# Counting two search rows in one packed pass, cutting GpSimd's projection low parts into pieces, and staging eleven weight tiles in block 0

## What is computed

```python
xn = layernorm(x)
s  = silu(xn @ Wg_a.T)
_, idx = top_k(-abs(s), k=1376)          # the half of each row nearest zero
s  = s.at[rows, idx].set(0.0)
s  = (s * (xn @ Wu_a.T)) @ Wd_a.T
g  = silu(((silu(xn @ Wg_b.T)) * (xn @ Wu_b.T)) @ Wd_b.T)
out = x + s * g
```

## Time and profile before

| | |
|---|---|
| median of 3 runs | 2782.26 us (2779.91 to 2783.34) |
| the profiled execution | 2784.59 us, its span 2782.8 us |
| TensorE busy in the span | 2753.9 us (99%) |
| VectorE busy | 2307.4 us (83%) |
| ScalarE busy | 1352.7 us (49%) |
| GpSimd busy | 388.3 us (14%) |
| mean granted clock | 0.996 |
| stages of block 0 on TensorE | A to 255.5 us, B to 489.5 us, BD to 608.4 us, AD from 613.0 us |

### The profile page before, as it was taken

The page is one execution under the profiler, slowest core; times in us unless marked ns, Lnnn a source line. Parts: engine busy times, 40 slices in busy tenths (PEclk is TensorE's granted clock), DMA queues, the critical chain, the costliest instruction groups (busy, mean ns, idle before and its releaser), DMA issues. The chain is left out here.

```text
span 2782.8 us, 31374 instructions
## 1 busy us (share of the span) xinstructions
PE 2753.9 (99%) x12204; PEld 2281.1 (82%) x12204; DVE 2307.4 (83%) x3002; ACT 1352.7 (49%) x1386; POOL 388.3 (14%) x161
## 2 busy tenths in 40 slices
PE   9999999999999999999999999999999999999999
PEld 7778888878788888888878888888887888888887
DVE  7676999999967698998986678999897767999971
ACT  4234998332444477631144557671115446776110
POOL 5565443044400000000020000000011000000000
PEclk9999999999999999999999999999999999999999
DMA  6898888579766555556656655555666664555564
GB/s 235 308 328 286 293 288 280 211 251 357 255 193 196 181 188 192 189 203 219 249 190 195 192 180 190 195 196 194 240 223 195 193 196 173 195 196 193 189 233 170
DMA packets 135097, 614.28 MB, mean 221 GB/s; under 512 B 12752, under 2 KB 12752, under 8 KB 89168
## 3 DMA queue, kind: packets, MB, share of 16 engines
q1 hardware_dynamic: 134992, 612.94, 63.2%
HBM read 492.31 MB, written 120.59 MB: 220 GB/s over the span
## 5 line engine op out<-in xcount | busy, mean ns | idle before, releaser
L632 PE MATMUL ps<-w_split,hid_ring 128*128 128x512 f32 x4096 | 935.2, 390 | 6.8 <-ACT hid_buf L1136 4.6
L632 PEld LDWEIGHTS ps<-w_split,hid_ring 128*128 128x128 f32 x4096 | 769.4, 188 | 171.5 <-issue 7.9
L1380 DVE TENSOR_SCALAR_CACHE_REDUCE ranks<-key_buf,cand 128x2752 int16<-128x2752 f32 x248 | 762.9, 3076 | 5.8
L961 ACT ACTIVATE signs_row<-key_buf,cand 128x2752 bf16<-128x2752 f32 x248 | 642.6, 2591 | 191.6 <-DVE cand L1389 182.0
L877 PE MATMUL ps<-xnT,w_split 128*128 128x512 f32 x1376 | 535.3, 389 | 0.0
L876 PE MATMUL ps<-xnT,w_split 128*128 128x512 f32 x1376 | 535.3, 389 | 0.0
L875 PE MATMUL ps<-xnT,w_split 128*128 128x512 f32 x1376 | 535.3, 389 | 0.0
L1206 POOL TENSOR_TENSOR w_split<-w_raw,w_split 128x1024 fp32r<-128x1024 f32 (+2 forms) x118 | 290.2, 2467 | 377.3 <-ACT w_split L928 137.0
L875 PEld LDWEIGHTS ps<-xnT,w_split 128*128 128x128 f32 x1376 | 258.3, 188 | 53.7
L876 PEld LDWEIGHTS ps<-xnT,w_split 128*128 128x128 f32 x1376 | 258.3, 188 | 53.6
L877 PEld LDWEIGHTS ps<-xnT,w_split 128*128 128x128 f32 x1376 | 258.3, 188 | 53.3
(11 more groups left out here) (146 smaller groups left out, 2907.0 us busy)
## 6 DMA issues: line engine op xcount, KB each, us to landing
w_split<-split SPq DMA_DIRECT2D x272, 1024.0 KB, 4.8
split<-w_split SPq DMA_DIRECT2D x72, 1024.0 KB, 6.8
w_raw<-w_a SPq DMA_DIRECT2D x100, 512.0 KB, 4.2
w_raw<-t_dram SPq DMA_DIRECT2D x78, 512.0 KB, 3.3
w_raw<-w_b SPq DMA_DIRECT2D x42, 512.0 KB, 4.9
w_extra_raw<-t_dram SPq DMA_DIRECT2D x42, 512.0 KB, 3.6
t_dram<-t_buf SPq DMA_DIRECT2D x20, 1024.0 KB, 8.6
w_extra_raw<-w_a SPq DMA_DIRECT2D x30, 512.0 KB, 3.6
```

Of the source, the lines that this page charges most:

```text
L632: ins = pe.matmul(ps[:, 2 * t + half, :], h, w[:, half * TB:(half + 1) * TB], start=(first and n == 0), stop=last and stop)
L961: act.activation(signs_row[:, :], keys[:, t, :], ACT.Sign, bias=cand_f[:, t:t + 1], scale=-1.0, accum_out=counts[:, t:t + 1]).then_inc(act ...
L1380: dve.tensor_scalar(ranks[:, :], keys[:, t, :], cand_f[:, t:t + 1], 0.0, ALU.is_lt, ALU.add, accum_out=counts[:, t:t + 1]).then_inc(sel_st ...
```

## The change

Three things are changed.

1. **Packed counts.** Row 0's comparison (key < candidate) writes 4096 or 0 into `ranks` and takes no sum. Row 1's comparison (key >= candidate) adds this to its own 1 or 0, in one `scalar_tensor_tensor` that takes the sum along. Two further steps of one column separate the two counts, by rounding to a multiple of 4096. `product_b` of a chunk moves from ahead of its first round into that round, between these steps and the wait for ScalarE's counts. The 31st round moves from BD into B: `TWO_AFTER` has nine chunks, (1, 3, 6, 8, 10, 12, 14, 16, 18), where it had eight.
2. **GpSimd in BD of block 0.** The low parts of BD's tiles are made in four pieces of 256 columns, and their waits for `hid_lo` (`LOWS_GATE`) are gone. In stage B the low parts stay whole, with their waits for `cand_ready`.
3. **Staging.** 11 tiles are staged where it were 14, one after every fourth tile of A where it was every third. So BD of block 0 splits 11 of its tiles itself, where it were 8.

```diff
-TWO_AFTER = (1, 4, 6, 9, 11, 14, 16, 19)
+TWO_AFTER = (1, 3, 6, 8, 10, 12, 14, 16, 18)
-LOWS_ROUND = 5
-assert ROUNDS_B + 1 == ROUNDS and LOWS_MASKS[-1][-1] == NJ
+assert ROUNDS_B == ROUNDS and LOWS_MASKS[-1][-1] == NJ
-STAGED = 14
-LOWS_GATE = {14: 14, 15: 14, 16: 15, 17: 18, 18: 18, 19: 19, 20: 19, 21: 22}
+STAGED = 11
 def stage_at(m):
-    s = (m - 3) // 3
-    return s if m % 3 == 0 and 0 <= s < STAGED else None
+    s = (m - 3) // 4
+    return s if m % 4 == 3 and 0 <= s < STAGED else None
...
-                    if j == 0:
-                        count(ROUNDS_B)
...
-                elif BD0 + STAGED <= m < AD0:
-                    pool.wait_ge(hid_lo, LOWS_GATE[m - BD0])
...
-                pool.tensor_tensor(w_lo[q][:, 0:w], w_raw[q][:, 0:w], w_hi[q][:, 0:w].bitcast(F32),
-                                   ALU.subtract).then_inc(lo_ready, 1)
+                piece = w // 4 if BD0 <= m < AD0 else w
+                for c in range(0, w, piece):
+                    cols = slice(c, c + piece)
+                    ins = pool.tensor_tensor(w_lo[q][:, cols], w_raw[q][:, cols], w_hi[q][:, cols].bitcast(F32), ALU.subtract)
+                ins.then_inc(lo_ready, 1)
...
-                def search_round(n):
+                def search_round(n, product=None):
...
-                    for t in range(DVE_ROWS):
-                        if t > 0:
-                            dve.wait_ge(sel_step, done + t)
-                        dve.tensor_scalar(ranks[:, :], keys[:, t, :], cand_f[:, t:t + 1], 0.0, ALU.is_lt, ALU.add,
-                                          accum_out=counts[:, t:t + 1]).then_inc(sel_step, 1)
-                    dve.wait_ge(sel_step, done + DVE_ROWS)
+                    dve.tensor_scalar(ranks[:, :], keys[:, 0, :], cand_f[:, 0:1], PACK, ALU.is_lt, ALU.mult).then_inc(sel_step, 1)
+                    dve.wait_ge(sel_step, done + 1)
+                    dve.scalar_tensor_tensor(out=ranks[:, :], in0=keys[:, 1, :], scalar=cand_f[:, 1:2], in1=ranks[:, :],
+                                             op0=ALU.is_ge, op1=ALU.add, accum_out=counts[:, 0:1]).then_inc(sel_step, 1)
+                    dve.wait_ge(sel_step, done + 2)
+                    dve.tensor_scalar(above[:, :], counts[:, 0:1], float(-(I // 2)), PACK_ROUND, ALU.add, ALU.add).then_inc(sel_step, 1)
+                    dve.wait_ge(sel_step, done + 3)
+                    dve.scalar_tensor_tensor(out=counts[:, 1:2], in0=above[:, :], scalar=PACK_ROUND, in1=counts[:, 0:1],
+                                             op0=ALU.subtract, op1=ALU.subtract).then_inc(sel_step, 1)
+                    if product is not None:
+                        product_b(product)
+                    dve.wait_ge(sel_step, done + 4)
                     dve.wait_ge(act_counted, b * (ROUNDS * ACT_ROWS) + n * ACT_ROWS + ACT_ROWS)
...
                 for c, rounds in enumerate(ROUNDS_AFTER):
-                    product_b(c)
                     for n in rounds:
-                        search_round(n)
+                        search_round(n, c if n == rounds.start else None)
...
                 lows_to(AHEAD + 1)
-                search_round(ROUNDS_B)
-                lows_to(LOWS_ROUND)
```

More of the change, by code:

```diff
@@ L76 @@
 DVE_ROWS = 2
+PACK = 4096.0
+PACK_ROUND = 1.5 * 2.0 ** 23 * PACK
+assert I < PACK and I // 2 < PACK / 2 and PACK * (I + 1) < 2 ** 24
 ACT_ROWS = NT - DVE_ROWS
@@ L341, in build @@
         need2 = small("need2", [1])
+        above = small("above", [1])
         found_f = found[:, :].bitcast(F32)
@@ L1267, in _ @@
             dve.memset(eps[:, :], EPS)
-            dve.memset(limits[:, 0:DVE_ROWS], K_ZERO - 0.5)
+            dve.memset(limits[:, 0:1], PACK * K_ZERO - 0.5)
+            dve.memset(limits[:, 1:2], K_ZERO - I - 0.5)
             dve.memset(limits[:, DVE_ROWS:NT], 2 * K_ZERO - I - 0.5).then_inc(consts, 1)
@@ L1337, in x_low @@
                                   ALU.subtract).then_inc(xn_ready, 1)
-            ROUND_STEPS = DVE_ROWS + 3
+            ROUND_STEPS = DVE_ROWS + 5
             CHECK_STEPS = ACT_ROWS + 2
@@ L1373, in run @@
             def run(b, last_block):
-                def search_round(n):
+                def search_round(n, product=None):
                     dve.wait_ge(cand_ready, b * (ROUNDS + 1) + n + 1)
                     done = b * (ROUNDS * ROUND_STEPS) + n * ROUND_STEPS
-                    for t in range(DVE_ROWS):
-                        if t > 0:
-                            dve.wait_ge(sel_step, done + t)
-                        dve.tensor_scalar(ranks[:, :], keys[:, t, :], cand_f[:, t:t + 1], 0.0, ALU.is_lt, ALU.add,
-                                          accum_out=counts[:, t:t + 1]).then_inc(sel_step, 1)
-                    dve.wait_ge(sel_step, done + DVE_ROWS)
+                    dve.tensor_scalar(ranks[:, :], keys[:, 0, :], cand_f[:, 0:1], PACK, ALU.is_lt, ALU.mult).then_inc(sel_step, 1)
[10 more added lines that the diff above has]
+                    dve.wait_ge(sel_step, done + 4)
                     dve.wait_ge(act_counted, b * (ROUNDS * ACT_ROWS) + n * ACT_ROWS + ACT_ROWS)
                     dve.tensor_tensor(accept[:, :], counts[:, :], limits[:, :], ALU.is_le).then_inc(sel_step, 1)
-                    dve.wait_ge(sel_step, done + (DVE_ROWS + 1))
+                    dve.wait_ge(sel_step, done + (DVE_ROWS + 3))
                     dve.tensor_scalar(bit[:, :], bit[:, :], 1, None, ALU.logical_shift_right).then_inc(sel_step, 1)
```

## The result

The changed kernel takes 2829.41 us (median of four, 2829.05 to 2830.58) against 2782.8 us beside it (median of four). One of these four executions took 4641.4 us and stands apart; without it the median is 2782.26, as in the table of before. The ratio is 1.017, interval 1.0157 to 1.0183: **slower by 47 us**, where 54 were forecast. The profiled execution took 2829.36 us, its span 2827.6.

A forecast was written before the change was run, and what follows sets the result against it. TensorE was taken to bound the kernel (busy 2753.9 of 2782.8 us), with VectorE setting the search's pace. 2784.6 + 58.9 - 3 - 2 = 2838.5, less 2.3 for the median: 2836 us; range 2770 to 2856.

The forecast's parts named there:

- Its main argument: Stage B, block 0: GpSimd's low parts hold both new VectorE passes, each adding 2.38 us to a round; stage +58.9 us.
- Prices: VectorE's search: first pass 1.62 us, second 3.12 with start; block 0 rounds 8.15, with product 8.84, with two low parts 11.0.
- Some twenty stops of 2 to 4 us: Sign in the new profile: TensorE in B of block 0 stops this often, each stop ending on GpSimd's low part.
- that pass takes the port first, the low part comes next, the second pass after it: Stage B, block 0: order of the first pass, GpSimd's subtraction and the second pass, as both start on the candidate.
- many second passes would take near 5.5: Sign in the new profile: second passes before 550 us often last 3.1 + 2.4 us, against 3.1 in blocks 1 to 3.
- BD and AD of block 0: Stages after B in block 0: the stop before AD shrinks by 2 to 3 us with its clock; -3, bounds -8.7 and +14.
- the last round leaves VectorE's order: BD of block 0: a 6.9 us round goes, VectorE is charged 15 us of holds against about 10 before; net -2.
- Stage A: Block 0's first stage: three subtractions fewer, three TensorE stops give back about 2 of their 5 us; bounds 0 and -7.
- (a): Stage B, block 0: only the first pass is held, so low parts hide behind the second; 2773 us, chance 0.21.
- (b): First pass keeps the old pace, 3.08 us; every block's B becomes VectorE-bound; 2845 us, chance 0.04.
- (c): Second pass, a `scalar_tensor_tensor`, runs at half pace in every block, 3 us more a round; about 3100 us, chance 0.04.
- (d): Block 0: low parts fall mostly into gaps, stage B grows by what BD gives back; within 0.2%, chance 0.05.

The follow-up runs named there:

- the memset: Changed kernel with GpSimd's subtraction in stage B of block 0 replaced by a memset of the low part to zero: 2776.07 us.
- the other kernel with the old stage A: Kernel before with the packed counts alone, old waits and whole low parts in BD, 14 staged tiles: 2832.94 us.
- the two kernels on the masks: Changed kernel with old counts in block 0, LOWS_CHECK 5 instead of 7: 2783.03 us; the same with a LOWS_MASKS step earlier too: 2784.04 us.

## Why the prediction was right

**Its main argument held.** That VectorE's new passes and GpSimd's low parts exclude each other, and that this makes stage B of block 0 bound by VectorE, is shown by the memset (234.0 us without the subtraction), by the packed counts alone (286.6 us) and by the old counts beside the same low parts (240.8 and 234.0 us). The stage was forecast at +58.9 us and came at +52.5.

**Prices.** First pass 1.62 forecast, 1.65 measured. Second pass 3.12 with its start, 3.13 measured from its start to that of the next step (3.08 by itself). Rounds 8.15, 8.84 and 11.0 forecast; 8.1, 8.6 and 10.6 measured. By the same counts, nine, ten and ten, these make 264.9 instead of 271.8, 6.9 too many: the product adds 0.5 to a round, not 0.69, and a second low part 2.0, not 2.19. Against this the last half tile ran at the lower clock and took 1.6 us more than the 2.7 forecast; small differences elsewhere make up the rest of the 6.4. "Some twenty stops of 2 to 4 us" were eighteen waits, nine of 2.3 us or more, with nine stretches at the lower clock between them.

**The order at the port was not as forecast.** The step "that pass takes the port first, the low part comes next, the second pass after it" failed. In 28 rounds the low part goes first, is held by nothing, and holds the first pass; the second pass is held only in the ten rounds with two low parts. One round was as forecast: the low part came 0.80 us behind the start of the first pass, which then took 1.66 us and wasn't held, and the low part took 3.1. I had said that many second passes would take near 5.5; ten take 5.1, and 29 of the 31 first passes are held, most to 3.84 or more. A round comes out nearly the same, since a low part excludes one pass in either order. The size was right with the order wrong, and that is in part luck.

**BD and AD of block 0: -3 forecast, +2.5 measured** (with A of block 1). Up to the start of AD it is +1.5 (125.0 against 123.5); the other 1.0 lies behind it, where kernels with the same code there range over 1.7 us (334.6 to 336.3). The step that failed is "the last round leaves VectorE's order", net -2. I took VectorE's sum of work as what ends the stage. The 6.9 us came back as 6.8 us of waits for ScalarE's high parts, which follow TensorE. VectorE is held 11.5 us, close to the 10 of before and not my 15; the last transposes end 122.8 us after BD's start, where they ended 121.2 us after it. The stop before AD grew from 5.0 to 6.1 us between starts, where I had it shrink by 2 to 3. It was inside the bounds (-8.7 to +14). The mask step set earlier took it to 1.8, so the places in the list decide it, not the sum alone.

**Stage A: -2 forecast, -7.5 measured,** just past the bound of -7, and -3.5 against the other kernel with the old stage A. The term was mis-sized: I gave back 2 of the 5 us of stops, and all of them went, with the clock behind them. The distance between staged tiles does it.

**Not forecast:** -2.7 us in the blocks behind, of which -1.3 and -1.5 lie in AD of blocks 1 and 2. Both kernels have a stop of 2.4 us there; behind it the kernel before has 3.4 us at the lower clock and the changed one hasn't. The kernel with pieces and staging alone has it in the one block and not in the other, and the two kernels on the masks differ in both with the same code there, so this can't be put down to the change.

**The rivals.** (a) the second pass isn't held: wrong. Wherever a low part meets it, in ten rounds, it takes 5.1 us instead of 3.08, and 3.45 and 4.0 beside pieces. That 21 of the 31 are undisturbed doesn't speak for it: the low part has gone by then, having held the first pass. (b) first pass at 3.08 and (c) second pass at half pace are refuted by 1.65 and 3.08 us in blocks 1 to 3. For (c), which went by the rule of the Trainium skill ("Vector Engine (DVE) Microarchitecture Reference", "Points that are easy to get wrong"), the chance was 0.04; with float32 and int16 sources and the sum taken along, 93 passes in the later blocks show 1.12 ns a column, the same as the old count with one source, so no halving against it. (d) gaps hide the low parts: not so, in 28 of 31 rounds a low part starts with the round's first pass.

## What to carry to other kernels

Before a VectorE pass is made faster, ask in which mode or with how many SBUF inputs the faster form runs, and what GpSimd does meanwhile: a pass made 1.4 us cheaper was held for 2.0 us, since its new form can't run beside a subtraction. If both must meet, cut GpSimd's operation, because a pass then waits for one piece at most; here quarters took back 28 of the 53 us of stage B, not all. Make sure too that a test kernel's own extra steps are small beside what it is to show: 0.21 us in each of 31 rounds comes to 6.5 us, nearly all of the 6.8 in question. And where work leaves a list whose steps wait for another engine, move the list's later steps forward too, or the time comes back as a wait.

## What the runs showed of the hardware

- GpSimd's low part, recorded 0.04 to 0.05 us after the first pass, still goes first (28 times); one recorded 0.80 us after it waits, and so does a memset recorded 0.18 us or more after it. What lies between 0.05 and 0.18 wasn't seen. So the recorded starts don't tell by themselves who has the port.
- With both engines queued they take turns, one instruction each: holds of 2.26, 1.14 and 0.59 us with pieces of 1024, 512 and 256 columns.
- A memset on GpSimd excludes the one-source pass (it then ends 0.89 us after it) and runs freely beside the two-source pass (0.95 us, as alone).
- Behind nine stops of stage B (most of them 3.2 us between starts, 27 us apart) the granted clock is at 1.2 GHz for 3.4 us. Behind stops of 2.4 us in AD of blocks 1 and 2 it is so in some executions and not in others with the same code there, and each time it adds 0.7 to 1.5 us. In a stage where VectorE sets the pace it adds nothing.
